# First two steps of a cross-attention kernel reordered around group 0: own weighing banks, split fc low part, first fc chunks ahead of group 1's shifts

## The reference

```python
x = layer_norm(hidden, ln1_w, ln1_b)
q, k, v = x @ q_w + q_b, enc @ k_w + k_b, enc @ v_w + v_b
scores = einsum('bhqd,bhkd->bhqk', q, k) / sqrt(16)      # masked
out = softmax(scores) @ v @ cproj_w + cproj_b
hidden = out + residual
y = gelu(layer_norm(hidden, ln2_w, ln2_b) @ fc_w + fc_b) @ proj_w + proj_b   # 256 -> 1024 -> 256
return hidden + y
```

## Time and profile before

| | us |
|---|---|
| median of 3 runs | 232.28 (230.33 to 232.5) |
| the profiled execution | 232.38 |
| its span, first to last instruction | 230.6 |
| TensorE busy, of the span | 214.9 (93%) |
| DVE busy | 176.0 (76%) |
| ACT busy | 125.7 (55%) |
| POOL busy | 90.7 (39%) |
| mean granted clock of TensorE | 0.985 |

### The profile page before, as it was taken

The page is one execution under the profiler, slowest core; times in us unless marked ns, Lnnn a source line. Parts: engine busy times, 40 slices in busy tenths (PEclk is TensorE's granted clock), DMA queues, the critical chain, the costliest instruction groups (busy, mean ns, idle before and its releaser), DMA issues.

```text
span 230.6 us, 8338 instructions
## 1 busy us (share of the span) xinstructions
PE 214.9 (93%) x3520; PEld 202.2 (88%) x3520; DVE 176.0 (76%) x378; ACT 125.7 (55%) x269; POOL 90.7 (39%) x101
## 2 busy tenths in 40 slices
PE   6978986878989999999999999999999999998995
PEld 6968976777979899999999999999999998897995
DVE  3678358866999796987979797979796779777571
ACT  3468357245923796169716972589248923651240
POOL 6345306528941195108621671248214611313300
PEclk9999798899999999999999999999999999999999
DMA  6958992950000483018500770079003900100101
GB/s 196 269 196 195 247 276 80 248 113 4 3 0 4 140 209 73 3 51 238 132 1 29 225 168 4 1 202 216 3 1 98 222 11 1 54 3 0 45 0 48
DMA packets 21980, 23.13 MB, mean 100 GB/s; under 512 B 1559, under 2 KB 20663, under 8 KB 21943
## 3 DMA queue, kind: packets, MB, share of 16 engines
q1 hardware_dynamic: 21008, 21.84, 37.3%
q10 hardware_dynamic: 934, 0.75, 1.1%
HBM read 7.62 MB, written 2.10 MB: 42 GB/s over the span
## 4 chain that ended last, share of the span: by engine, by line
PE 69%; DVE 11%; DMA 8%; issue 6%; ACT 2%; POOL 1%; SPq 1%; POOLq 0%; ACTq 0%
PE bank L1071 19%; PE bank L1072 16%; PE bank L1073 16%; PE bank L1149 6%; DMA stack_kq<-n_t 4%; DMA ctx_in<-in_ctx_t 4%; PE scores L1131 3%; PE scores L1101 3%; DVE recip L875 3%; PE bank L1088 3%; PE bank L1216 2%; DVE z L917 1%; POOL rs L560 1%; DVE mx L830 1%; DVE g_hi L892 1%
## 5 line engine op out<-in xcount | busy, mean ns | idle before, releaser
L1071 PE MATMUL bank<-proj_hi,g_hi 128*128 128x256 f32 x128 | 38.2, 299 | 2.4 <-DVE g_lo L894 2.4
L1071 PE MATMUL bank<-z_hi,fc_hi 128*128 128x256 f32 x128 | 37.5, 293 | 0.0
L1072 PE MATMUL bank<-z_hi,fc_lo 128*128 128x256 f32 x128 | 36.0, 281 | 0.0
L1072 PE MATMUL bank<-proj_hi,g_lo 128*128 128x256 f32 x128 | 36.0, 281 | 0.0
L1073 PE MATMUL bank<-proj_lo,g_hi 128*128 128x256 f32 x128 | 36.0, 281 | 0.0
L1073 PE MATMUL bank<-z_lo,fc_hi 128*128 128x256 f32 x128 | 35.9, 281 | 0.0
L875 DVE RECIPROCAL recip<-bank 128x256 f32<-128x256 f32 x16 | 28.0, 1751 | 5.1 <-PE bank L1149 5.1
L560 POOL TENSOR_TENSOR rs<-ve,power 128x1 f32<-128x1 f32 x16 | 9.9, 616 | 53.3 <-DVE ve L855 53.3
L631 ACT ACTIVATE fc_raw<-bank,fc_bias 128x256 f32<-128x256 f32 x64 | 26.7, 471 | 6.4 <-PE bank L1073 6.3
L1071 PEld LDWEIGHTS bank<-proj_hi,g_hi 128*128 128x128 f32 x128 | 24.1, 188 | 4.6 <-DVE g_lo L894 4.1
L830 DVE TENSOR_REDUCE mx<-scores 128x16 f32<-128x1024 f32 x16 | 19.5, 1220 | 10.3 <-PE scores L1101 10.3
(11 more groups left out here) (126 smaller groups left out, 586.9 us busy)
## 6 DMA issues: line engine op xcount, KB each, us to landing
stack_kq<-parts SPq DMA_DIRECT2D x48, 256.0 KB
x_in<-in_x SPq DMA_DIRECT2D x8, 256.0 KB, 3.3
ctx_in<-in_ctx_t SPq DMA_DIRECT2D x7, 256.0 KB, 3.4
out<-y SPq DMA_DIRECT2D x7, 256.0 KB, 2.1
fc_raw<-in_fc_w SPq DMA_DIRECT2D x1, 1024.0 KB, 9.3
proj_raw<-in_proj_w SPq DMA_DIRECT2D x1, 1024.0 KB, 9.8
ctx_in<-in_ctx_t ACTq DMA_DIRECT2D x1, 256.0 KB, 4.0
w_raw_q<-in_q_w SPq DMA_DIRECT2D x1, 256.0 KB, 4.7
```

Of the source, the lines that this page charges most:

```text
L1071: mm(out_ap, a_hi, b_hi, start=first, stop=False, skip_group_check=True)
L1072: mm(out_ap, a_lo, b_hi, start=False, stop=False, skip_group_check=True)
```

## The change

- **Weighing banks.** `weigh_bank` gives half 1 of g0 bank4 of its own, all others bank7 as before. The ones products of a `weigh` become four matmuls of 256 columns at its start instead of 16 of 64; those with v stay.
- **Both outputs first.** On DVE both `outputs` of g0 follow each other; `maxima(a, 0)` comes after the first `hidden`, and `maxima(a, 1)`, `left_q(g2)` move to the first full step, ahead of `rest_of_z2`. On PE both `weigh` of g0 come ahead of `first_score(a)`, and both `project` ahead of `turn_maxima(a, 0)`; `make_v(g2)` moves to the first full step.
- **fc's parts.** The high part signals each half; the low part is made in two halves, one ahead of `maxima(b, 0)` and one ahead of `maxima(b, 1)`.
- **fc's column sums** move behind the bias product, half ahead of and half behind `turn_maxima(b, 1)`, and `shift(b, 0)` follows; `make_q(g2)` comes between the two shifts.
- **DMAs.** g1's last two part DMAs wait for the maxima DMA of half 0 of g0, and the proj load for that of half 1.
- **POOL.** `x_and_bias(a)` comes between the two `row_scale`; `third_q(g2)` moves to the first full step.
- **First full step.** PE does `turn_z2`, `turn_maxima(b, 1)`, `fc_chunk` 0, `shift(b, 0)`, `fc_chunk` 1, `shift(b, 1)`, `weigh(b, 0)`, `make_v`. On ACT `high_of_z2` comes first and `second_q(g2)` between the exps. `turn_maxima` and `outputs` get waits on `o_made`.

```diff
--- before.py
+++ after.py
@@ -324,6 +324,12 @@
     def is_last(g):
...
+    def weigh_bank(g, p):
...
+        if g.c == 0 and p:
+            return bank4.rearrange("p w (k t) -> p w k t", k=KC)
+        return bank7
@@ -357,6 +363,8 @@
         def stack_parts(g):
...
             for k in range(PARTS):
+                if g.c == 1 and k == PARTS - 1:
+                    sp.wait_ge(n_stacked[0], 16)
@@ -383,6 +391,7 @@
             stack_parts(a)
+            sp.wait_ge(n_stacked[1], 16)
@@ -507,12 +516,11 @@
             third_k(Group(0, 2))
-            third_q(Group(0, 2))
...
             row_scale(b, 0)
+            x_and_bias(a)
             row_scale(b, 1)
-            x_and_bias(a)
@@ -520,7 +528,7 @@
         def full_step(a, b, c, ahead=True):
...
                 third_k(a)
-                third_q(a)
+            third_q(a)
@@ -727,31 +735,34 @@
             act.wait_ge(w_loaded["fc"], 16)
-            scaled_high("fc", fc_hi, fc_raw, "ln2_w")
+            for k in range(KC):
+                sc.activation(fc_hi[:, k, :], fc_raw[:, k, :], ACT.Copy,
+                              scale=col[:, COLS["ln2_w"] + k:COLS["ln2_w"] + k + 1]).then_inc(w_high["fc"], 1)
+            keep_v(a, zeroed=True)
...
             stack_maxima(b, 0)
-            keep_v(a, zeroed=True)
+            lead_k(Group(0, 2))
...
             high(w_hi["c"], w_raw["c"], w_high["c"])
-            lead_k(Group(0, 2))
+            second_k(Group(0, 2))
             exp(b, 0)
+            exp(b, 1)
             lead_q(Group(0, 2))
-            exp(b, 1)
-            second_k(Group(0, 2))
-            second_q(Group(0, 2))
             o_lead(b, 0)
-            keep_maxima(a, 0)
-            stack_maxima(a, 0)
...
             high(proj_hi, proj_raw, w_high["proj"])
+            keep_maxima(a, 0)
+            stack_maxima(a, 0)
...
         def full_step(a, b, c, ahead=True):
             fetch_table(ACT.Exp)
-            if not first_full(c):
+            if first_full(c):
+                high_of_z2(c)
+            else:
@@ -760,9 +771,8 @@
                 second_k(a)
-            high_of_z2(c)
-            if not first_full(c):
-                second_q(a)
+                high_of_z2(c)
+            second_q(a)
@@ -872,10 +882,11 @@
         def outputs(g, p):
...
             dve.wait_ge(weighed, g.count(2, p + 1))
-            ve.reciprocal(recip[:], bank7[:, 1, :, :]).then_inc(recip_made, 1)
+            wait(dve, o_made, g.count(2, p))
+            ve.reciprocal(recip[:], weigh_bank(g, p)[:, 1, :, :]).then_inc(recip_made, 1)
...
             wait(dve, o_split, g.count(2, p))
-            ve.tensor_tensor(o[:], bank7[:, 0, :, :], recip[:], ALU.mult).then_inc(o_made, 1)
+            ve.tensor_tensor(o[:], weigh_bank(g, p)[:, 0, :, :], recip[:], ALU.mult).then_inc(o_made, 1)
@@ -938,6 +949,12 @@
             ve.tensor_tensor(z2_lo[:], bank0[:], z2_hi[:].bitcast(F32), ALU.subtract).then_inc(z2_split, 1)
...
+        def rest_of_fc(k):
+            dve.wait_ge(w_high["fc"], k + 1)
+            ve.scalar_tensor_tensor(fc_lo[:, k, :], fc_raw[:, k, :],
+                                    col[:, COLS["ln2_w"] + k:COLS["ln2_w"] + k + 1],
+                                    fc_hi[:, k, :].bitcast(F32), ALU.mult, ALU.subtract).then_inc(w_split["fc"], 1)
@@ -977,25 +994,23 @@
             normal1(Group(0, 2))
+            rest_of_fc(0)
+            maxima(b, 0)
+            rest_of_fc(1)
+            maxima(b, 1)
+            left_k(Group(0, 2))
+            rest_of_z(Group(0, 2))
...
                              ALU.add).then_inc(bias_ready, 1)
-            maxima(b, 0)
-            maxima(b, 1)
-            rest_of_z(Group(0, 2))
-            dve.wait_ge(bias_summed, 3)
...
                              ALU.add).then_inc(bias_ready, 1)
-            rest_of_scaled("fc", fc_lo, fc_raw, fc_hi, "ln2_w")
-            left_k(Group(0, 2))
-            left_q(Group(0, 2))
             outputs(b, 0)
-            maxima(a, 0)
...
             variance2(b, 0)
-            maxima(a, 1)
+            maxima(a, 0)
@@ -1004,8 +1019,9 @@
             normal2(c, 1)
-            if not first_full(c):
-                left_q(a)
+            if first_full(c):
+                maxima(b, 1)
+            left_q(a)
@@ -1106,6 +1122,8 @@
         def turn_maxima(g, p):
             pe.wait_ge(n_split, g.count(2, p + 1))
+            if g.c == 1 and p == 0:
+                pe.wait_ge(o_made, 2)
@@ -1138,17 +1156,21 @@
         def weigh(g, p):
...
             pe.wait_ge(exped, g.count(4, 2 * p + 2))
-            wait(pe, o_made, g.count(2, p))
+            if g.c == 0:
+                pe.wait_ge(n_kept, 2)
+            else:
+                pe.wait_ge(o_made, g.count(2, p))
+            for i in range(4):
+                mm(weigh_bank(g, p)[32 * i:32 * i + 32, 1, :, :], ones_bd[:].rearrange("p w d -> p (w d)"),
+                   probs[p][:, i:HP:4, :, :].rearrange("p h b q -> p h (b q)"),
+                   start=True, stop=True, skip_group_check=True)
...
                 for b in range(2):
-                    cols_b = slice(S * b, S * b + S)
-                    for kind in range(2):
-                        for i in range(4):
-                            hp = 4 * half + i
-                            w = ones_bd[:] if kind else v_bd[g.slot][:, 2 * p + b, hp, :, :]
-                            last = mm(bank7[32 * i:32 * i + 32, kind, half, cols_b],
-                                      w.rearrange("p w d -> p (w d)"), probs[p][:, hp, b, :],
-                                      start=True, stop=True, skip_group_check=True)
+                    for i in range(4):
+                        hp = 4 * half + i
+                        last = mm(weigh_bank(g, p)[32 * i:32 * i + 32, 0, half, S * b:S * b + S],
+                                  v_bd[g.slot][:, 2 * p + b, hp, :, :].rearrange("p w d -> p (w d)"),
+                                  probs[p][:, hp, b, :], start=True, stop=True, skip_group_check=True)
@@ -1264,12 +1286,8 @@
             make_q(a)
-            pe.wait_ge(w_loaded["fc"], 16)
-            pe.wait_ge(bias_ready, 1)
-            column_sums(bank7[:, 1, 0, 0:MB], fc_raw, "ln2_b", range(MB)).then_inc(bias_summed, 1)
...
             make_v(a, 1)
-            keep_clock(scores[:, 0, 0:P], 12)
@@ -1279,61 +1297,69 @@
             pe.wait_ge(vb_repeated, 1)
-            pe.wait_ge(bias_ready, 2)
+            pe.wait_ge(bias_ready, 1)
             for k in range(KC):
-                last = mm(bank7[:, 0, :, :].rearrange("p k t -> p (k t)"), vb_rep[:, k, :], w_raw["c"][:, k, :],
-                          start=(k == 0), stop=(k == KC - 1), skip_group_check=True)
-            last.then_inc(bias_summed, 1)
+                mm(bank7[:, 0, :, :].rearrange("p k t -> p (k t)"), vb_rep[:, k, :], w_raw["c"][:, k, :],
+                   start=(k == 0), stop=(k == KC - 1), skip_group_check=True)
+            pe.wait_ge(w_loaded["fc"], 16)
+            column_sums(bank7[:, 1, 0, 0:MB], fc_raw, "ln2_b", range(MB // 2))
+            turn_maxima(b, 1)
+            column_sums(bank7[:, 1, 0, 0:MB], fc_raw, "ln2_b", range(MB // 2, MB)).then_inc(bias_summed, 1)
+            shift(b, 0)
             pe.wait_ge(q_left, 2)
-            keep_clock(bank5[:, 0, 0:P], 14)
-            turn_maxima(b, 1)
-            keep_clock(bank5[:, 0, 0:P], 14)
             make_q(Group(0, 2))
-            shift(b, 0)
-            shift(b, 1)
...
             pe.wait_ge(bias_ready, 3)
+            shift(b, 1)
             weigh(b, 0)
+            keep_clock(bank5[:, 0, 0:P], 10)
+            weigh(b, 1)
...
             first_score(a)
-            keep_clock(bank5[:, 0, 0:P], 10)
-            weigh(b, 1)
-            make_v(Group(0, 2), 0)
+            keep_clock(bank6[:, 0, 0:P], 12)
             pe.wait_ge(w_split["c"], 1)
+            project(b, 0, a)
+            keep_clock(bank6[:, 0, 0:P], 20)
+            project(b, 1, a)
+            keep_clock(bank6[:, 0, 0:P], 10)
             turn_maxima(a, 0)
-            project(b, 0, a)
             score(a, 1)
-            make_v(Group(0, 2), 1)
-            pe.wait_ge(q_left, 3)
-            keep_clock(bank1[:, 0, 0:P], 20)
-            project(b, 1, a)
-            keep_clock(bank1[:, 0, 0:P], 14)
+            keep_clock(bank6[:, 0, 0:P], 14)
...
         def full_step(a, b, c, ahead=True):
-            if not first_full(c):
+            if first_full(c):
+                pe.wait_ge(k_left, a.count(1, 1))
+                turn_z2(c)
+                keep_clock(bank6[:, 0, 0:P], 16)
+                pe.wait_ge(n_kept, 3)
+                turn_maxima(b, 1)
+                pe.wait_ge(n_kept, 4)
+                pe.wait_ge(z2_split, c.count(1, 1))
+                pe.wait_ge(w_split["fc"], KC)
+                fc_chunk(c, 0)
+                shift(b, 0)
+                pe.wait_ge(hid_made, c.count(2, 2))
+                fc_chunk(c, 1)
+                shift(b, 1)
+                weigh(b, 0)
+                make_v(a, 0)
```

(29 more changed lines are left out.)

## The result

The changed kernel takes **241.17 us** (median, 240.61 to 242.0) against 231.8 us before on the same chip: ratio 1.0397, 95% interval 1.0362 to 1.0433, slower by 9.4 us. The profiled execution took 240.65 us with a span of 238.8 us, against 232.38 and 230.6.

What follows compares the result with a forecast made beforehand. TensorE was taken as the bound from 57.2 us on, so only time ahead of the first full step's end counts. (57.5 − 57.17) + 5.0 − 0.9 = +4.4, plus 0.1 for the clock, on 232.38 gave 236.9 us, range 231.0 to 239.5.

Steps and rivals of the forecast that it cites:

- Won up to z: 4.0 us: Second step: the moves and quicker DMA end the second row scale at 49.4 instead of 53.43, 4.0 us won.
- proj_lo behind the last row scale holds z to its end: Second step: GpSimd's 4.62 us operation holds VectorE's z for half 1, which ends at 54.15 instead of 49.8.
- lock lost: Rival, 20 in 100: z for half 1 gets in ahead of proj_lo or isn't held; say 232.0 us.
- three terms: Sum under lock lost: T earlier −4.1, first GELU later after T +5.0, idle time filled −0.9, total 0.0 us.
- z's end to T: 3.3: First full step: VectorE's maxima(b, 1), left_q(Group 2) and z_lo stand behind z, 3.3 us, so T is 57.5.
- T: Start of group 0's first fc chunk, fc_chunk(c, 0), in the first full step: 57.17 before, 57.5 forecast.
- T to the first GELU's end: 7.7: First full step: GELU waits behind group 1's shifts and exps, ending at T + 7.7 instead of T + 2.64; 5.0 added.
- the GELU's end to `make_k`: 13.9: First full step: 14.8 us before, less 0.98 of TensorE's idle time that a later GELU fills, leaves 13.9.
- weigh: 0: All 16 weighings: fewer, wider ones products change nothing, as bursts wait for columns, whose number stays the same.
- The waits on SP do their work: Second step: group 0's maxima DMA takes 3.45 us instead of 6.12; rival that it doesn't: 238.2, 9 in 100.
- xb between the row scales: half of 0.5: Second step: POOL's xb(a) can hold the last small operation of maxima(a, 0) by 0.5 us; half taken.

Runs made afterwards that it cites:

- kernel with two undone: Changed kernel with proj's low part behind z's split and fc's column sums whole, back in the wait of the second step's start: 232.95 us, ratio 1.0013.
- the kernel with v's product moved: The kernel with two undone, with group 2's v product back in the second step in place of clock-keeping products: 235.28 us, ratio 1.0125.
- the run with xb behind both: Changed kernel with x_and_bias(a) again behind both row scales, as before the change: 241.82 us, ratio 1.0441.
- the run with GpSimd's two operations late: Kernel before, with GpSimd's second x plus bias and proj's low part waiting until z is split: 236.99 us, ratio 1.0169.

## Why the prediction was wrong

It gave 236.9 us with a range to 239.5; 241.17 came. The direction was right, and so was the mechanism of the held `z`. The sum was 3.8 us short on the profiled execution (240.65), and 3.0 of that is one term.

- **Won up to z: 4.0 us. This is the step that failed.** Measured 1.0. The sum had `shift(b, 0)` at 34.4, `weigh(b, 0)` at 38.6, the last row scale ended at 49.4; they were at 36.45, 41.26 and 52.45. Two thirds of the 3 us arise up to `shift(b, 0)`: 0.6 up to the turn of the first maxima (29.48 for 28.9; the first scores waited to 26.07, not 25), 0.5 in the scores and the bias product, and 1.0 in the column sums, 4.6 us where I put 3.6, from a row at the higher clock. The 3.6 are what they took in the run with `proj_lo` late, at the higher clock (31.49 to 35.13). I saw that they were last here ("not the DMA") and priced `make_q` at the lower clock, but not the sums themselves. The lower clock was there in parts of 17.9 to 21.3, in 27.5 to 30.9 and from 34.3 to 41.2; before only in 24.7 to 28.1 and 38.3 to 41.7. In 34.3 to 37.7 the granted clock is 0.50 to 0.90 in all six profiles with the sums in the new place, and 1.00 in all eight with them in the old one. Whether the emptied wait lowers it or the sums themselves do wasn't separated. Moving the sums back gave 2.5 to 4 us alone and 3.8 with `proj_lo` late. Of the last 1.0 us, 0.6 are group 0's two shifts, 1.0 us each at the lower clock where I had 0.7. The rest is in small pieces; the largest is 0.2, `o_hi` of half 1 starting only behind the first `project` (47.15, `o` ended at 46.95).
- **proj_lo behind the last row scale holds z to its end.** Right: 4.58 us, to 0.15 us behind GpSimd's end. Freed, it gives 5.1 us; with half the piece, half. The rival "lock lost" is out. Its price, 232.0 us, would have been wrong too: `z` free and the sums in the new place is the run with `proj_lo` late, 236.15 us, short by the same term. The kernel with two undone has its three terms (I had −4.1 + 5.0 − 0.9 = 0.0, measured −4.0 + 5.1 − 1.1), but with the sums moved back; that they meet is partly luck.
- **z's end to T: 3.3.** Measured 3.6, but by another path: I added up VectorE's operations, and the last of them, `z_lo`, ends at 60.00. T waits for the second maxima's copy on ScalarE (60.62), behind `turn_z2` and 16 clock-keeping products at the lower clock (57.21 to 59.80). That 3.3 came near is luck.
- **T to the first GELU's end: 7.7.** Measured 8.2; the first chunk took 2.06 instead of 1.43, at the lower clock; **the GELU's end to `make_k`: 13.9**, measured 13.8.
- **weigh: 0.** Right within −2.1 to +0.4 us, shown alone: 24 instructions fewer of 64 in each weighing made no difference that this run can measure. The Trainium skill ("TensorEngine Tiling (Array Packing)", "Instruction Overhead") has about 60 cycles for each matmul, 25 ns at 2.4 GHz. By it, as an estimate, six instructions fewer in each column group would save 0.15 us in each of the 14 weighings on the path, 2.1 us in all, the very end of that interval. The forecast held 14 ns for each instruction against these 60 cycles, but that is a mean over four overlapping groups; within one it is 56 ns, so the rows don't speak against them, and this case doesn't decide it.
- **The waits on SP do their work.** proj's load landed in 5.7 us instead of 9.8, and the maxima's rows were no longer what `shift(b, 0)` waited for. Worth nothing in the changed kernel, where `shift(b, 0)` starts behind the sums without a wait. With the sums moved back it starts at 33.08, 3.4 us ahead of the landing before (30.41 + 6.12 = 36.53), so there the quicker DMA was needed; it wasn't tried by itself.
- **xb between the row scales: half of 0.5.** The small operation took 0.74 instead of 0.17, so 0.57, above the 0.5 that I gave as the most.

The range was too narrow on the side of the clock. I gave 0.8 us for it, from one chunk; it bears on every TensorE row of the second step.

The rule in the Trainium skill ("SBUF — State Buffer", "Who interferes with whom"), that the first of VectorE and GpSimd keeps the shared port for its whole instruction, agrees with 2.33 and 2.42, 4.49 and 4.58.

Open: why the kernel with v's product moved lost 1.1% more than its mechanism explains. In its profile the first scores are late ahead of the edit, with TensorE's clock at 0.60 in 17.9 to 21.3 us against 1.00 in the kernel with two undone. Why the clock was lower there, and whether that is chance or an effect of the edit, wasn't separated.

## What to carry to other kernels

Work that stands in a wait is free only there: ask where it goes and what waits in its new place, and price it at the clock of that place, for both levels if the rows show both. When a long GpSimd operation holds a VectorE operation, list every VectorE operation that could stand beside it before moving it: the hold isn't removed but handed to the next of its kind, and it costs what goes beyond that one's slack. Giving one group the right of way wins up to the first point where the engines take both groups in order; here ScalarE's exponentials ahead of the GELU cost 5 us again.

## What the runs showed that I had not expected

- A VectorE operation of 16 elements a partition with bf16 output (0.17 us) was held for 3.23 us, and one of 2 elements for 3.69, as fully as one of 256. A cast was held too (2.78, free 0.41). `TENSOR_REDUCE` beside the same GpSimd operation kept its 1.21 us (54.20 in the run with xb behind both), and so did `RECIPROCAL` its 1.74 (57.55 in the run with GpSimd's two operations late).
- Products of one column feel the clock as wide ones do: 32 of the column sums take 3.46 us, 0.11 each; 16 of them, partly at the lower clock, 2.88 us, 0.18 each.
- With identical code up to 30 us, the first scores start at 25.61 in one profile and at 28.32 and 28.39 in two others. TensorE didn't wait longer: at 28.39 the sums and v's product ahead took 4.2 and 2.8 us instead of 3.5 and 1.8, at the lower clock. This is as large as most effects studied here.
